# Conditional tiles as the last chunk of each expert, and one 512-column product for both parts of w2

## The chip, the core and the metric

The kernel runs on one core of one Trainium2 chip. The metric is device time in microseconds (us) of one launch. The time before is 896.36 us, the median of three runs (894.65 to 896.64).

## The reference

Two layers are computed and both results go into one output. The first is an RWKV-style attention block with a layer norm ahead of it; the second, with which the change has to do, is a mixture of experts behind another layer norm, whose result is added to the first layer's:

```python
h1 = jnp.einsum('ebcm,emh->ebch', dispatch, w1)
h3 = jnp.einsum('ebcm,emh->ebch', dispatch, w3)
expert_out = jnp.einsum('ebch,ehm->ebcm', jax.nn.silu(h1) * h3, w2)
final = jnp.einsum('ebcm,bsec->bsm', expert_out, combine_mask)
```

There are 8 experts, hidden size 256 (C), inner size 896 (F, 7 groups of 128), 4096 tokens, 2 experts for each token and room for 1280 rows (10 tiles of 128) in each expert. Everything is float32 on the outside.

## The kernel before

The program has two phases, written for five engines by hand, each as a list of instructions with semaphores. Phase A does the attention block, the router and the dispatch of rows to a buffer in HBM (`disp`), and the up products of expert 0's early tiles. Phase B (`phase_b`) does the experts.

**Precision.** A float32 product is made of three products of the type float32r: each operand is split into a high part and a low part (what is left over), and high x high, high x low and low x high are summed in PSUM. The weights of the next expert are split while this one is computed: ScalarE casts a piece of the raw weight `wraw` to the high part (`split_hi`, L1597), GpSimd subtracts for the low part (`split_lo`, L1540). There are 4 pieces (WP) for each of w1, w3 and w2, the matrices m = 0, 1 and 2.

**Tiles and chunks.** The 10 tiles of an expert lie in three chunks, `CHUNKS = [(0, 2), (2, 4), (6, 4)]` (first tile, number of tiles). Chunk 0 holds the last 256 rows of an expert's room. It is *conditional*: a count of the rows that the expert has (`taken`) is read into a register, and the chunk's up products are passed over where no row reaches it; its two down tiles are each decided in the same way (`where_taken`, L1440 to L1447). Where an arm is not taken the engine instead raises the semaphores that others wait for (`pass_over`). In the profiled execution experts 1, 3 and 5 take the chunk, with one down tile each.

**One expert on TensorE** (`step`, L1887). First the turn (transpose) of the conditional rows and `up(e, 0)`, if taken; then `up(e, 1)`, `down_rest(e, 0)` (the conditional down tiles), `up(e, 2)`, `down_chunk(e, 1)`, and `last_chunk(e)`: the four down tiles of chunk 2, with the turns of the next expert's rows between them. `up(e, c)` (L1802) makes 7 groups f of 12 products for w1 and w3, 512 columns wide in chunks 1 and 2 and 256 in chunk 0. `down(e, t)` (L1822) makes 21 products of 256 columns, three for each f:

```python
nc.tensor.matmul(py[j % 2][:, 0:C], a, hi[:, cut], start=(f == 0), stop=False)
nc.tensor.matmul(py[j % 2][:, 0:C], a, lo[:, cut], start=False, stop=False)
ins = nc.tensor.matmul(py[j % 2][:, 0:C], b, hi[:, cut], start=False, stop=(f == FT - 1))
```

**Behind the up products** stand, for each f, silu on ScalarE (`gated`, L1611), the product with the w3 half on VectorE (`hid`, L1734), its high part on ScalarE (`hh`, L1620) and its low part on VectorE (`hl`, L1742). `down` waits for the last low part of its chunk. Behind a down tile ScalarE scales it by the router's weight (`scale_out`, L1633) into one of four buffers `ysb`, and GpSimd adds it to the output with an indirect DMA (`add`, L1548).

**Expert 0** (`first`, L1874) starts with chunk 1, whose up products are in phase A: three down tiles, the turns of chunk 2's rows, the fourth down tile, then chunk 0 if taken, `up(e, 2)`, `down_rest`, `last_chunk`.

**Transfers.** SyncE's queue (`on_sync`, L1492) brings for the next expert, in this order: w1 and w3 (each when its buffer of `wraw` has been split), the rows `xtok` (when the turns of this expert's rows are all made or passed over: the semaphore `turned`; L1500), and w2 (L1507).

Of the kernel before, what the change touches and what calls it, by code (L numbers as in the profile page):

```python
# [161 lines left out]
def build(nc, x, maa, decay_row, decay_ch, u_row, wrT, wkT, wvT, wgT, woT, lnw, lnb, gateT, w1, w2, w3, out):  # L162
    disp = nc.dram_tensor("disp", [E * SLOTS, ROW], F32).ap()
    persist = ExitStack()
    with persist:
# [20 lines left out]
        whi = [[sb(f"whi0_{m}", [P, NW], F32R) for m in range(3)]]  # L186
        wlo = [[sb(f"wlo0_{m}", [P, NW], F32R) for m in range(3)]]
# [3 lines left out]
        with ExitStack() as ctx:  # L191
            first = phase_a(nc, *tensors(ctx), ctx, sem, ident, x, maa, decay_row, decay_ch, u_row, (wrT, wkT, wvT, wgT, woT),
                            lnw, lnb, gateT, disp, out, whi[0], wlo[0], wraw, expert_views(w1, w3, w2), taken, kept)
        with ExitStack() as ctx:
            sb2, ps2 = tensors(ctx)
            whi.append([sb2(f"whi1_{m}", [P, NW], F32R) for m in range(3)])
            wlo.append([sb2(f"wlo1_{m}", [P, NW], F32R) for m in range(3)])
            second = phase_b(nc, sb2, ps2, ctx, sem, ident, whi, wlo, wraw, w1, w2, w3, taken, disp, out, kept)
# [55 lines left out]

def expert_views(w1, w3, w2):
# [5 lines left out]
def phase_a(nc, sb, ps, ctx, sem, ident, x, maa, decay_row, decay_ch, u_row, weights, lnw, lnb, gateT, disp, out,  # L261
            whi, wlo, wraw, first_w, taken, kept):
# [160 lines left out]
    def piece_cut(i):  # L423
        return slice(i % WP * WPC, (i % WP + 1) * WPC)

# [45 lines left out]
    def on_gpsimd(pool):  # L471
# [76 lines left out]
        def weight_low(i):  # L548
            if 0 <= i < NPIECE:
                m, cut = i // WP, piece_cut(i)  # L550
                pool.wait_ge(whi_ready, i + 1)
                nc.gpsimd.tensor_tensor(wlo[m][:, cut], wraw[m % 2][:, cut], whi[m][:, cut].bitcast(F32),
                                        ALU.subtract).then_inc(wlo_ready, 1)
# [61 lines left out]
    def on_scalar(act):  # L615
# [108 lines left out]
        def weight_high(i):  # L724
            if 0 <= i < NPIECE:
                m, cut = i // WP, piece_cut(i)
                act.wait_ge(w_in[m % 2], 16 * (m // 2 + 1))
                nc.scalar.copy(whi[m][:, cut], wraw[m % 2][:, cut]).then_inc(whi_ready, 1)
# [413 lines left out]
    def on_tensor(pe):  # L1142
# [177 lines left out]
        def early_up(f):  # L1320
# [7 lines left out]
            for m, dst in ((0, early_p1[f % 2]), (1, early_p3[f % 2])):  # L1328
                for kt in range(KT):
                    wcut = slice(kt * F + f * P, kt * F + (f + 1) * P)  # L1330
                    nc.tensor.matmul(dst, whi[m][:, wcut], kept.xh[:, kt, early_cols], start=(kt == 0), stop=False)
                    nc.tensor.matmul(dst, whi[m][:, wcut], kept.xl[:, kt, early_cols], start=False, stop=False)
                    ins = nc.tensor.matmul(dst, wlo[m][:, wcut], kept.xh[:, kt, early_cols], start=False, stop=(kt == KT - 1))
# [68 lines left out]
def phase_b(nc, sb, ps, ctx, sem, ident, whi, wlo, wraw, w1, w2, w3, taken, disp, out, kept):  # L1402
# [17 lines left out]
    ffn_done, ysb_ready = sem("ffn_done"), sem("ysb_ready")  # L1420
# [34 lines left out]
    def run(eng, first, step):  # L1455
# [474 lines left out]
```

## Time and profile before

| | |
|---|---|
| median of 3 runs | 896.36 us |
| the profiled execution: its own time | 896.49 us |
| the profiled execution: span from first to last instruction | 894.8 us |
| TensorE (PE) busy | 846.2 us |
| ScalarE (ACT) busy | 489.2 us |
| VectorE (DVE) busy | 472.9 us |
| GpSimd (POOL) busy | 467.1 us |
| mean granted TensorE clock | 0.992 of full speed |

The span is shorter than the execution's own time by what lies ahead of the first and behind the last instruction. Phase B begins on TensorE at 364.71 us. PE is the row of matmuls, PEld that of weight loads, which overlap them; a name with a q behind it (PEldq, SPq) is the engine's sequencer or queue. A matmul's own duration includes time in which the next one already streams, so products are compared by the distance of their starts.

### The profile page before, as it was taken

Reading aid. Unit: us, or ns where it says so; the run is one execution under the profiler, and the core shown is the slowest. Engines: PE = TensorE matmul, PEld = TensorE weight load, DVE = VectorE, ACT = ScalarE, POOL = GpSimd, SP = SyncE. Lnnn points to the kernel's source line nnn. Section 1 sums busy time; section 2 is a strip of 40 time slices with the busy share of each in tenths; the row PEclk is TensorE's granted clock in tenths of the full one; section 3 lists DMA queues with packets and bytes.
Section 4 is the critical chain, followed back from the end, with each engine's and each line's share of the span. In section 5 each row is a group of like instructions: output and inputs, shape, how many; then the busy total and the mean of one; then the engine's idle time right before and its main releaser. Section 6 shows DMA issues by size and latency. Waiting matters only on the chain. (4 is left out here: it accounts for less than half of the span.)

```text
span 894.8 us, 18307 instructions
## 1 busy us (share of the span) xinstructions
PE 846.2 (95%) x6791; PEld 705.4 (79%) x6791; DVE 472.9 (53%) x1173; ACT 489.2 (55%) x876; POOL 467.1 (52%) x497
## 2 busy tenths in 40 slices
PE   3999999999999999889999999999999999999995
PEld 2777777777777777779889889879789889889885
DVE  6788788788888766343441442442351443342430
ACT  4578787777777779263542443443452444453331
POOL 4434766777767675564337355237346137447014
PEclk9999999999999999999999999999999999999998
DMA  5852132112111121546116236025417024314013
GB/s 154 320 193 67 50 102 67 62 56 80 38 38 38 38 98 53 170 150 139 42 42 118 86 92 111 5 78 89 112 48 137 22 72 92 82 42 54 7 19 42
DMA packets 50465, 73.93 MB, mean 83 GB/s; under 512 B 5056, under 2 KB 42176, under 8 KB 50368
## 3 DMA queue, kind: packets, MB, share of 16 engines
q1 hardware_dynamic: 35488, 53.46, 18.0%
q0 software_dynamic: 14592, 19.18, 12.5%
q8 instruction: 60, 0.98, 0.5%
q14 instruction: 37, 0.30, 0.1%
q10 hardware_dynamic: 288, 0.01, 0.0%
HBM read 38.41 MB, written 34.22 MB: 81 GB/s over the span
## 5 line engine op out<-in xcount | busy, mean ns | idle before, releaser
L1540 POOL TENSOR_TENSOR wlo<-wraw,whi 128x448 fp32r<-128x448 f32 x84 | 107.1, 1278 | 201.5 <-ACT whi L1597 201.5
L1817 PE MATMUL p<-xh,whi 128*128 128x512 f32 (+1 forms) x504 | 190.4, 378 | 7.3 <-DVE xl L1716 4.7
L1819 PE MATMUL p<-xh,wlo 128*128 128x512 f32 (+1 forms) x504 | 189.7, 376 | 0.0
L1818 PE MATMUL p<-xl,whi 128*128 128x512 f32 (+1 forms) x504 | 189.3, 376 | 0.0
L1734 DVE TENSOR_TENSOR hid<-gated,p 128x512 f32<-128x512 f32 (+1 forms) x126 | 81.1, 644 | 204.3 <-ACT gated L1611 204.3
L1548 POOL DMA_INDIRECT out<-ysb,index x80 | 126.0, 1575 | 85.2 <-ACT ysb L1633 55.1
L1611 ACT ACTIVATE gated<-p 128x512 f32<-128x512 f32 (+1 forms) x126 | 70.8, 562 | 179.7 <-PE p L1819 179.7
L1837 PE MATMUL py<-whi,hh 128*128 128x256 f32 x469 | 135.1, 288 | 6.2 <-DVE hl L1742 3.1
L1839 PE MATMUL py<-whi,hl 128*128 128x256 f32 x469 | 132.8, 283 | 0.0
L1838 PE MATMUL py<-wlo,hh 128*128 128x256 f32 x469 | 132.5, 283 | 0.0
L1817 PEld LDWEIGHTS p<-xh,whi 128*128 128x128 f32 x504 | 94.7, 188 | 27.4 <-DVE xl L1716 5.4
L1819 PEld LDWEIGHTS p<-xh,wlo 128*128 128x128 f32 x504 | 94.8, 188 | 19.0
L1818 PEld LDWEIGHTS p<-xl,whi 128*128 128x128 f32 x504 | 94.7, 188 | 18.7
L1633 ACT ACTIVATE ysb<-py,weight 128x256 f32<-128x256 f32 x67 | 31.7, 474 | 120.8 <-PE py L1839 100.8
L1837 PEld LDWEIGHTS py<-whi,hh 128*128 128x128 f32 x469 | 89.3, 190 | 7.3 <-DVE hl L1053 3.5
L927 DVE TENSOR_TENSOR attm<-pS,dmask 128x512 f32<-128x512 f32 x128 | 79.4, 682 | 27.8 <-PE pS L1218 23.5
L1742 DVE TENSOR_TENSOR hl<-hid,hh 128x512 fp32r<-128x512 f32 (+1 forms) x126 | 88.9, 706 | 3.7 <-ACT hh L1620 3.1
L1838 PEld LDWEIGHTS py<-wlo,hh 128*128 128x128 f32 x469 | 89.1, 190 | 0.4
L1839 PEld LDWEIGHTS py<-whi,hl 128*128 128x128 f32 x469 | 89.0, 190 | 0.0
L1716 DVE TENSOR_TENSOR xl<-pt,xh 128x512 fp32r<-128x512 f32 x33 | 22.7, 691 | 111.0 <-ACT xh L1603 111.0
L567 POOL DMA_INDIRECT disp<-row,slot_i x64 | 65.0, 1015 | 31.3 <-issue 14.3
L1620 ACT CAST hh<-hid 128x512 fp32r<-128x512 f32 (+1 forms) x126 | 72.8, 578 | 1.1 <-DVE hid L1734 1.1
(192 smaller groups left out, 1441.1 us busy)
## 6 DMA issues: line engine op xcount, KB each, us to landing
wraw<-in_w SPq DMA_DIRECT2D x24, 896.0 KB
disp<-wraw SPq DMA_DIRECT2D x16, 662.5 KB, 9.2
xtok<-disp SPq DMA_DIRECT2D x16, 530.0 KB, 4.5
x_ring<-in_x SPq DMA_DIRECT2D x16, 256.0 KB, 3.0
out<-x SPq DMA_DIRECT2D x16, 256.0 KB
xtok<-disp SPq DMA_DIRECT2D x8, 265.0 KB, 6.1
out<-ysb,index POOLq DMA_INDIRECT x80
disp<-row,slot_i POOLq DMA_INDIRECT x64
```

The lines of the kernel that those rows point to most:

```text
L927: nc.vector.tensor_tensor(attm[g][:], pS[:, :, g // 2, g % 2, :], group_mask(g), ALU.mult).then_inc(attm_ready[g], 1)
L1540: nc.gpsimd.tensor_tensor(wlo[e.const % 2][m][:, cut], wraw[k][:, cut], whi[e.const % 2][m][:, cut].bitcast(F32), ALU.subtract).then_inc(w ...
L1548: nc.gpsimd.indirect_dma_start(out, bass.IndirectOffsetOnAxis(ap=index[e.const % 2][:, t:t + 1], axis=0), ysb[j % NY][:], None, compute_op ...
L1620: nc.scalar.copy(hh[(u * NCH + q) % 2][:, f, 0:w], hid[k][:, 0:w]).then_inc(hh_ready, 1)
L1734: nc.vector.tensor_tensor(hid[k][:, 0:w], gated[k][:, 0:w], p3[k][:, 0:w], ALU.mult).then_inc(hid_ready, 1)
L1742: nc.vector.tensor_tensor(hl[s][:, f, 0:w], hid[k][:, 0:w], hh[s][:, f, 0:w].bitcast(F32), ALU.subtract).then_inc(hl_ready, 1)
L1817: nc.tensor.matmul(dst[:, 0:w], hi[m][:, wcut], xh[xcut], start=(kt == 0), stop=False)
L1818: nc.tensor.matmul(dst[:, 0:w], hi[m][:, wcut], xl[xcut], start=False, stop=False)
L1819: ins = nc.tensor.matmul(dst[:, 0:w], lo[m][:, wcut], xh[xcut], start=False, stop=(kt == KT - 1))
L1837: nc.tensor.matmul(py[j % 2][:, 0:C], a, hi[:, cut], start=(f == 0), stop=False)
L1838: nc.tensor.matmul(py[j % 2][:, 0:C], a, lo[:, cut], start=False, stop=False)
L1839: ins = nc.tensor.matmul(py[j % 2][:, 0:C], b, hi[:, cut], start=False, stop=(f == FT - 1))
```

## The change

Three things change, all in phase B's order and in how w2 is kept.

1. w2's high and low parts lie side by side (`Split.w2`, 128 x 7 x 2 x 256). In the tiles that are not conditional one product of 512 columns multiplies the high hidden values with both; the product of the low hidden values with the high weights stays. PSUM holds two halves of 256 columns. ScalarE scales the half with the low weights into `ysb` (semaphore `low_ready`), and VectorE multiplies the other half by the weight and adds it (`sum_out`, new). The conditional tiles keep three products and ScalarE alone.
2. In experts 0 to 6 the order of chunks is 1, 2, 0: `up(e, 1)`, the decision, in both of its arms `up(e, 2)` and the down tiles of chunk 1 (in the taken arm with the turn of the conditional rows ahead and `up(e, 0)` behind), `last_chunk(e)`, and `down_rest(e, 0)` last. The last expert keeps the order 0, 1, 2. ScalarE, VectorE and GpSimd follow.
3. In expert 0 two early down tiles instead of three stand ahead of the turns, one behind them, and the fourth behind `up(e, 2)`.

The pieces of w2 are cut through all 7 groups, 64 columns of each, where they were 448 contiguous ones. SyncE's list of transfers is the same.

```diff
--- before.py
+++ after.py
@@ -75,7 +75,7 @@
 def chunk_order(e):
 
-    return [EARLY, *(c for c in range(NCH) if c != EARLY)] if e.reg is None and e.const == 0 else list(range(NCH))
+    return [1, 2, 0] if e.const < E - 1 else [0, 1, 2]
...
+class Split:
+
+
+
+    def __init__(self, sb, k):
+        self.up = [[sb(f"w{part}{k}_{m}", [P, NW], F32R) for m in range(2)] for part in ("hi", "lo")]
+        self.w2 = sb(f"w2_{k}", [P, FT, 2, C], F32R)
+
+    def piece(self, part, m, q):
+
+        if m < 2:
+            return self.up[part][m][:, q * WPC:(q + 1) * WPC]
+        return self.w2[:, :, part, q * (C // WP):(q + 1) * (C // WP)]
+
+
+def raw_piece(raw, m, q):
+
+    if m < 2:
+        return raw[:, q * WPC:(q + 1) * WPC]
+    return raw[:].rearrange("p (f c) -> p f c", c=C)[:, :, q * (C // WP):(q + 1) * (C // WP)]
...
             j = ST * pair(e)[1] + q
             e.wait(pool, ysb_ready, ST, q + 1)
             pool.wait_ge(rows_in[0], 16)
+            if q == ST - REST and t < REST:
+
+                added_before(pool, e, ST // 2)
             nc.gpsimd.indirect_dma_start(
                 out, bass.IndirectOffsetOnAxis(ap=index[e.const % 2][:, t:t + 1], axis=0),
                 ysb[j % NY][:], None, compute_op=ALU.add).then_inc(added[j % NY], 16)
...
-            nc.scalar.activation(ysb[j % NY][:], py[j % 2][:, 0:C], ACT.Copy, scale=weight[e.const % 2][:, t:t + 1]).then_inc(ysb_ready, 1)
+            by = weight[e.const % 2][:, t:t + 1]
+            if t < REST:
+                e.wait(act, ysb_ready, ST, q)
+                nc.scalar.activation(ysb[j % NY][:], py[j % 2][:, 0:C], ACT.Copy, scale=by).then_inc(ysb_ready, 1)
+            else:
+                nc.scalar.activation(ysb[j % NY][:], py[j % 2][:, C:2 * C], ACT.Copy, scale=by).then_inc(low_ready, 1)
...
+        def sum_out(e, t):
+
+            q = tile_at(e, t)
+            j = ST * pair(e)[1] + q
+            e.wait(dve, low_ready, COMMON, t - REST + 1)
+            nc.vector.scalar_tensor_tensor(ysb[j % NY][:], py[j % 2][:, 0:C], weight[e.const % 2][:, t:t + 1], ysb[j % NY][:],
+                                           ALU.mult, ALU.add).then_inc(ysb_ready, 1)
+
...
-            hi, lo = whi[e.const % 2][2], wlo[e.const % 2][2]
+            w2, to = split[e.const % 2].w2, py[j % 2]
             for f in range(FT):
                 a, b = hh[s][:, f, off:off + P], hl[s][:, f, off:off + P]
-                cut = slice(f * C, (f + 1) * C)
-                nc.tensor.matmul(py[j % 2][:, 0:C], a, hi[:, cut], start=(f == 0), stop=False)
-                nc.tensor.matmul(py[j % 2][:, 0:C], a, lo[:, cut], start=False, stop=False)
-                ins = nc.tensor.matmul(py[j % 2][:, 0:C], b, hi[:, cut], start=False, stop=(f == FT - 1))
+                if t < REST:
+                    nc.tensor.matmul(to[:, 0:C], a, w2[:, f, 0, :], start=(f == 0), stop=False)
+                    nc.tensor.matmul(to[:, 0:C], a, w2[:, f, 1, :], start=False, stop=False)
+                    ins = nc.tensor.matmul(to[:, 0:C], b, w2[:, f, 0, :], start=False, stop=(f == FT - 1))
+                else:
+                    if f:
+                        nc.tensor.matmul(to[:, 0:C], b, w2[:, f, 0, :], start=False, stop=False)
+                    ins = nc.tensor.matmul(to[:], a, w2[:, f].rearrange("p h c -> p (h c)"), start=(f == 0), stop=(f == FT - 1))
+                    if not f:
+                        nc.tensor.matmul(to[:, 0:C], b, w2[:, f, 0, :], start=False, stop=False)
             ins.then_inc(ffn_done, 1)
 
         def down_chunk(e, c):
...
+        def with_rest_where_taken(e, between):
+
+
+            def up_rest():
+                turn(e, TB - 1)
+                between()
+                up(e, 0)
+
+            def no_rest():
+                pass_over(pe, e, (turned, TB - 1, TB, 1))
+                between()
+                pass_over(pe, e, (h_done, chunk_at(e, 0) * FT, HPE, FT))
+
+            where_taken(pe, e, COMMON, up_rest, no_rest)
 
...
         def first(e):
             t0, n = CHUNKS[EARLY]
-            for t in range(t0, t0 + n - 1):
+            for t in range(t0, t0 + n - 2):
                 down(e, t)
             for i in range(2, TB - 1):
                 turn(e, i)
-            down(e, t0 + n - 1)
+            down(e, t0 + n - 2)
             pe.wait_ge(taken_ready, 1)
-            rest_where_taken(e)
-            up(e, 2)
+
+            def second():
+                up(e, 2)
+                down(e, t0 + n - 1)
+
+            with_rest_where_taken(e, second)
+            last_chunk(e)
             down_rest(e, 0)
+
+        def step(e):
+            up(e, 1)
+
+            def second():
+                up(e, 2)
+                down_chunk(e, 1)
+
+            with_rest_where_taken(e, second)
             last_chunk(e)
-
-        def step(e):
+            down_rest(e, 0)
+
+        def last(e):
             rest_where_taken(e)
             up(e, 1)
             down_rest(e, 0)
@@ -1892,7 +2030,7 @@
             down_chunk(e, 1)
             last_chunk(e)
 
-        run(pe, first, step)
+        run(first, step, last)
```

The places that the prediction speaks of, in TensorE's list. First the start of expert 1, with the decision on the conditional chunk (L1443/L1444, in the change L1460/L1461). In the names p1 and p3 are the PSUM banks of the up products, py those of the down products, pt those of the turns. Before:

```order
L1838 MATMUL py1<-wlo0_2,hh0 128x256
L1839 MATMUL py1<-whi0_2,hl0 128x256
L1443 TENSOR_LOAD taken
L1444 COMPARE_AND_BRANCH
L1799 MATMUL pt1<-ident,xtok 128x128 [waits xl_ready,rows_in2]
L1799 MATMUL pt1<-ident,xtok 128x128 x3
L1817 MATMUL p1_1<-xh,whi1_0 128x256 [waits hid_ready,wlo_ready,xl_ready]
```

The change:

```order
L1920 MATMUL p3_1<-xl,whi1_1 128x512
L1921 MATMUL p3_1<-xh,wlo1_1 128x512
L1460 TENSOR_LOAD taken
L1461 COMPARE_AND_BRANCH
L1901 MATMUL pt1<-ident,xtok 128x128 [waits xl_ready,rows_in2]
L1901 MATMUL pt1<-ident,xtok 128x128 x3
L1919 MATMUL p1_0<-xh,whi1_0 128x512 [waits hid_ready,wlo_ready,xl_ready]
```

The decision has moved from behind the previous expert's down products to behind chunk 1's up products, and the products that follow the turn are chunk 2's of 512 columns, where they were the conditional ones of 256. This arm now also holds the down tiles of chunk 1 and `up(e, 0)`.

Next, the end of the conditional down tiles, `pass_over` with its wait for ffn_done. Before, in expert 1, between `up(e, 1)` and `up(e, 2)`:

```order
L1837 MATMUL py1<-whi1_2,hh1 128x256
L1838 MATMUL py1<-wlo1_2,hh1 128x256
L1839 MATMUL py1<-whi1_2,hl1 128x256
L1444 UNCONDITIONAL_BRANCH
L1446 UNCONDITIONAL_BRANCH [waits ffn_done] x2
L1817 MATMUL p1_1<-xh,whi1_0 128x512 [waits hid_ready,wlo_ready,xl_ready]
```

The change, at the end of expert 6 (behind its `last_chunk`), where the last expert's decision follows at once:

```order
L1940 MATMUL py1<-w2_0,hh0 128x256
L1941 MATMUL py1<-w2_0,hl0 128x256
L1461 UNCONDITIONAL_BRANCH
L1463 UNCONDITIONAL_BRANCH [waits ffn_done] x2
L1460 TENSOR_LOAD taken
L1461 COMPARE_AND_BRANCH
L1901 MATMUL pt1<-ident,xtok 128x128 [waits xl_ready,rows_in2]
L1901 MATMUL pt1<-ident,xtok 128x128 x3
```

The wait for ffn_done now stands behind the last product of the expert; behind experts 0 to 5 the next expert's `up(e, 1)` follows it, behind expert 6 the second decision.

## Rows read from the trace of the kernel before

**Rows 1.** The page's busy time of each engine (share of the span, instructions).
```profile
PE 846.2 (95%) x6791; PEld 705.4 (79%) x6791; DVE 472.9 (53%) x1173; ACT 489.2 (55%) x876; POOL 467.1 (52%) x497
```
**Rows 2.** Timeline of PE, expert 0: start, duration; in brackets the idle time before, releaser.
```profile
364.71 0.39 PE L1837 MATMUL py<-whi,hh 128*128 128x256 f32 x1 [3.04 <-DVE hl L1053]
...
377.11 0.28 PE L1839 MATMUL py<-whi,hl 128*128 128x256 f32 x1
377.98 0.47 PE L1817 MATMUL p<-xh,whi 128*128 128x512 f32 x1 [0.59 <-DVEq L1453]
...
401.30 0.39 PE L1837 MATMUL py<-whi,hh 128*128 128x256 f32 x1 [3.11 <-DVE hl L1742]
```
**Rows 3.** The same, first conditional product of experts 1 and 5 (first and last of three).
```profile
414.82 0.39 PE L1817 MATMUL p<-xh,whi 128*128 128x256 f32 x1 [1.55 <-DVE xl L1716]
...
690.32 0.39 PE L1817 MATMUL p<-xh,whi 128*128 128x256 f32 x1 [1.57 <-DVE xl L1716]
```
**Rows 4.** The same, first product of up(2) behind a conditional down tile, experts 1 and 5.
```profile
447.82 0.47 PE L1817 MATMUL p<-xh,whi 128*128 128x512 f32 x1 [0.54 <-POOL wlo L1540]
...
723.31 0.47 PE L1817 MATMUL p<-xh,whi 128*128 128x512 f32 x1 [0.53 <-POOL wlo L1540]
```
**Rows 5.** TensorE's reads of the register (taken) near 375 and 625, and a product behind.
```profile
L1443 PEldq TENSOR_LOAD <-taken x1: 497/497/497, 375.1 to 375.1; - x1
...
L1443 PEldq TENSOR_LOAD <-taken x1: 308/308/308, 624.7 to 624.7; - x1
...
627.26 0.47 PE L1817 MATMUL p<-xh,whi 128*128 128x512 f32 x1 [0.28 <-DVEq L1453]
```
**Rows 6.** Timeline of PE, 26 steps between down products, 20 between up products.
```profile
879.76 0.28 PE L1837 MATMUL py<-whi,hh 128*128 128x256 f32 x1
...
882.85 0.28 PE L1839 MATMUL py<-whi,hl 128*128 128x256 f32 x1
...
392.70 0.39 PE L1817 MATMUL p<-xh,whi 128*128 128x512 f32 x1
...
397.35 0.40 PE L1819 MATMUL p<-xh,wlo 128*128 128x512 f32 x1
```
**Rows 7.** Groups by line and shape (count, busy us, mean ns, idle before).
```profile
L908 DVE SCALAR_TENSOR_TENSOR mixed<-diff,maa_sb,xT 128x256 f32<-128x256 f32 x96 | 53.7, 613 | 0.0
L1734 DVE TENSOR_TENSOR hid<-gated,p 128x256 f32<-128x256 f32 x21 | 8.8, 421 | 19.9 <-ACT gated L1611 19.9
...
L1633 ACT ACTIVATE ysb<-py,weight 128x256 f32<-128x256 f32 x67 | 31.7, 474 | 120.8 <-PE py L1839 100.8 <-DMA out<-ysb,index 18.1 <-issue 1.9
```
**Rows 8.** Timeline, ACT's and POOL's last instructions.
```profile
885.30 0.47 ACT L1633 ACTIVATE ysb<-py,weight 128x256 f32<-128x256 f32 x1 [2.02 <-PE py L1839]
886.05 1.55 POOL L1548 DMA_INDIRECT out<-ysb,index  x1 [0.94 <-ACT ysb L1633]
```
**Rows 9.** Timeline of ACT and DVE behind the last up product of expert 0.
```profile
398.79 1.03 ACT L1597 CAST whi<-wraw 128x448 fp32r<-128x448 f32 x2
399.72 0.62 ACT L1620 CAST hh<-hid 128x512 fp32r<-128x512 f32 x1
400.37 0.87 DVE L1742 TENSOR_TENSOR hl<-hid,hh 128x512 fp32r<-128x512 f32 x1 [0.67 <-ACT hh L1620]
```
**Rows 10.** Landing of the row loads of 413 (three), the densest stretch, w2's first piece.
```profile
DMA to landing us min/median/max: 3.9/5.0/6.1
...
368.00:379.00 11.00, 10.40 (x80) 10.05 (x80) 1.44 (x4) 2.93 (x6) 5.53 (x4) 0.95 0.95 276
...
460.30 0.57 ACT L1597 CAST whi<-wraw 128x448 fp32r<-128x448 f32 x1
```
**Rows 11.** The page's DMA queues: instructions (packets, MB, share of 16 engines).
```profile
q8 instruction: 60, 0.98, 0.5%
```
**Rows 12.** Windows: busy us of PE, PEld, DVE, ACT, POOL, granted clock, DMA share, GB/s.
```profile
366.00:369.00 3.00, 3.00 (x16) 3.00 (x16) 0.00 (x0) 0.23 (x1) 0.00 (x1) 0.50 0.17 51
401.00:404.00 3.00, 2.70 (x22) 2.70 (x23) 0.85 (x2) 0.00 (x0) 2.81 (x2) 1.00 0.21 29
```

More of the change, by code:

```diff
@@ L185, in build @@
         kept = Kept(nc, sb)
[L186 to L187 removed]
+        split = [Split(sb, 0)]
         wraw = [sb(f"wraw{k}", [P, NW]) for k in range(2)]
@@ L725, in weight_high @@
             if 0 <= i < NPIECE:
-                m, cut = i // WP, piece_cut(i)
+                m, q = i // WP, i % WP
                 act.wait_ge(w_in[m % 2], 16 * (m // 2 + 1))
-                nc.scalar.copy(whi[m][:, cut], wraw[m % 2][:, cut]).then_inc(whi_ready, 1)
+                nc.scalar.copy(split.piece(0, m, q), raw_piece(wraw[m % 2], m, q)).then_inc(whi_ready, 1)
         def turned1(b):
@@ L1453, in pass_over, with run @@
             eng.sem_inc(s, by)
-    def run(eng, first, step):
+    def run(first, step, last):
         first(At(0))
-        step(At(1))
-        for e in range(2, E):
+        for e in range(1, E - 1):
             step(At(e))
+        last(At(E - 1))
     def banks():
@@ L1578, in step @@
             added_before(pool, e, 0)
-            for t in range(ST):
+            for q, t in enumerate(tile_order(e)):
                 add(e, t)
-                if t == ST - 3 and (e + 1).valid(E):
+                if q == ST - 3 and (e + 1).valid(E):
                     keep_index(e + 1)
-        run(pool, first, step)
+        run(first, step, step)
         added_before(pool, At(E), 0)
@@ L1596, in split_hi @@
                 e.wait(act, ffn_done, ST, -ST)
-            nc.scalar.copy(whi[e.const % 2][m][:, cut], wraw[(3 * u + m) % 2][:, cut]).then_inc(whi_ready, 1)
+            nc.scalar.copy(split[e.const % 2].piece(0, m, q), raw_piece(wraw[(3 * u + m) % 2], m, q)).then_inc(whi_ready, 1)
         def turn_hi(e, i):
@@ L1708, in free_hidden @@
             past.wait(eng, ffn_done, ST, tiles_done(past, q % NCH))
-        run(act, first, step)
+        run(first, step, last)
     def on_vector(dve):
@@ L1775, in first, with second, last @@
             dve.sem_inc(rows_used, 1)
-            rest_where_taken(e)
-            hidden(e, 2)
-            next_rows(e + 1)
-        def step(e):
+            def second():
+                hidden(e, 2)
+                sum_out(e, t0 + n - 1)
+            with_rest_where_taken(e, second)
+            last_chunk(e, True)
+        def step(e):
+            hidden(e, 1)
+            def second():
+                hidden(e, 2)
+                sum_chunk(e, 1)
+            with_rest_where_taken(e, second)
+            last_chunk(e, True)
+        def last(e):
             rest_where_taken(e)
@@ L1783, in step @@
             hidden(e, 2)
-            if (e + 1).valid(E):
-                next_rows(e + 1)
-        run(dve, first, step)
+            sum_chunk(e, 1)
+            last_chunk(e, False)
+        run(first, step, last)
     def on_tensor(pe):
@@ L1875, in first @@
             t0, n = CHUNKS[EARLY]
-            for t in range(t0, t0 + n - 1):
+            for t in range(t0, t0 + n - 2):
                 down(e, t)
@@ L1893, in step @@
             last_chunk(e)
-        run(pe, first, step)
+        run(first, step, last)
     return on_sync, on_gpsimd, on_scalar, on_vector, on_tensor
```

115 lines of the change are left out of this document (77 added, 38 removed).

## The prediction

> **What bounds the kernel now.** I read the engine shares of the page first. They show TensorE busy 95% of the span and no other engine above 55% [rows 1], so time can come only from TensorE's products or from its gaps. Next I read TensorE's own order of time for what stands in brackets behind a product, which is the gap before it. In the second phase these gaps are few. Expert 0 waits 3.11 us for the last low part of the hidden values before its last four tiles [rows 2]. Each of the three experts that take the conditional tiles (1, 3 and 5) waits 1.55 to 1.57 us for VectorE's xl before the first conditional product [rows 3]. After the one conditional down tile that each of them has, TensorE drains and restarts with 0.53 to 0.54 us lost in the first and the last of them [rows 4]. Two more places lose 0.59 and 0.28 us behind a decision that is read but not taken [rows 2, 5]. Then I took the pitch of products from start to start: 26 products of 256 columns take 3.09 us, 118.9 ns each; 20 of 512 columns take 4.65 us, 232.5 ns each [rows 6].
>
> **Part 1: one 512-column product.** A down tile has 7 triples of 256-column products; the 64 tiles that are not conditional become 7 pairs, one of 256 columns and one of 512. The columns streamed are the same 768. A triple costs 3 x 118.9 = 356.6 ns, a pair 118.9 + 232.5 = 351.4 ns: 5.2 ns less, and 448 of them give **2.3 us**. No row shows the two widths in turn. One bound is no gain, if the time goes by columns alone. The other comes from the slope of the same rows: (232.5 - 118.9) / 256 = 0.444 ns a column, 768 columns at that are 341 ns, which would give 15.8 ns x 448 = 7.1 us. I take 2.3, because it uses each width's own row. The Trainium skill (TensorE: Matmul & The Clock Gate, "Back-to-back issue gap") gives a gap of N/2.4 + 2.5 ns, so dropping one product of three would save 2.5 ns a triple and 1.1 us in all; its gaps of 109 and 216 ns are shorter than both measured pitches, so I keep the rows.
>
> The price is a VectorE step: ScalarE scales the low half (256 columns, 474 ns as before), VectorE multiplies the high half from PSUM and adds. The nearest VectorE rows are 421 ns for a two-input product and 613 ns for a scalar-tensor-tensor of this size [rows 7]; I take 0.5. For 63 of the 64 tiles it is hidden: a tile takes 2.5 us, its two PSUM banks alternate, and 0.47 + 0.5 us with two hand-overs are over long before the tile after next begins. Queued behind it on VectorE are the next expert's turned rows and weights, which have a tile's time each. Without that cover each tile would lose 0.6 us. At the very end there is no cover: ScalarE's scale at 885.30 released the last scatter at 886.05 [rows 8], and VectorE now stands between. That costs 0.5 + 0.1 = **0.6 us**.
>
> **Part 2: the order in expert 0.** Its last early tile moves behind the second chunk's up products. The wait of 3.11 us is a chain behind the last up product: silu, two weight pieces (1.03 us), the high part at 399.72, the low part at 400.37 [rows 9]. None of that gets shorter, but 21 products (2.5 us) now lie inside it. About 0.6 us stays. Gain **2.5 us**.
>
> **Part 3: the conditional tiles last (experts 0 to 6).** The turn of the conditional rows now has chunk 2's up products and chunk 1's down products (30 us) between it and its use, so the three gaps of rows 3 go: **4.7 us**. They are replaced as follows.
>
> - The down part of the conditional chunk now ends each expert. Not taken, it waits for the expert's own last product (ffn_done) before the next expert's up products can be issued. The same wait costs 0.53 to 0.54 us in the taken case today [rows 4]. Taken experts keep it; experts 0, 2 and 4 are new: 3 x 0.54 = **1.6 us lost**. The existing 0.28 us [rows 5] goes into it: 0.3 gained.
> - Between experts 6 and 7 two decisions follow each other, because the last expert keeps the old order. The second is read only after the first has drained TensorE. From the reading of the register to the next product rows show 377.98 - 375.1 = 2.9 us [rows 2, 5] and 627.26 - 624.7 = 2.6 us [rows 5]. Today TensorE's queue hides most of this; here the queue is empty. **2.7 us lost**.
> - The decision after up(1) is hidden. The read at 375.1 is 17 products ahead of the last one issued (377.1, 118.9 ns apart); at 512 columns 17 products are 3.9 us, more than 2.9.
> - At the end of a taken arm TensorE jumps over the other arm, under 256-column products, with only 2 us of queue. I put 0.1 us on each of three: **0.3 us**, below by nothing.
> - Transfers: the rows of expert e+1 are requested only after up(1), and w2 of e+1 stands behind them in SyncE's queue. Rows need 3.9 to 6.1 us to land; the densest stretch moved 276 GB/s, so rows and w2 together (2.2 MB) need some 8 to 9 us and are there about 10 us into up(2) at worst [rows 10]. The first piece of w2 is taken 12.5 us into up(2) (447.82 to 460.30) [rows 4, 10]. Hidden by some 2.5 us.
> - GpSimd issues the two conditional scatters after the others, 1.55 us each [rows 8]. Behind them stand the next expert's low weight parts, which start two up groups (5.6 us) later. Its new wait for this expert's first five scatters asks for ones issued over 10 us before: nothing.
> - The pieces of w2 are now cut in runs of 64 elements on ScalarE and GpSimd. If GpSimd took half as long again, its four pieces would still end before the down products that read them. Nothing.
>
> **The sum.** Gains 2.3 + 2.5 + 4.7 + 0.3 = 9.8; losses 0.6 + 1.6 + 2.7 + 0.3 = 5.2; net 4.6 us. The profiled execution took 896.49 us (span 894.8), so 891.9; it lies 0.13 above the median of the three runs, so 891.8 us.
>
> **Rivals.**
> (A) *The wide product gives nothing* because only columns count. For: columns are unchanged, and the pitch of both widths is near proportional. Against: the intercept of rows 6 is positive. 891.8 + 2.3 = **894.1 us**.
> (B) *Long jumps become visible: slower.* The arms now hold the second chunk's up and down products, so that the decision of experts 1 to 6 jumps over 226 products where it jumped over 88, and a taken arm ends by jumping over 140 where it jumped over none. If the instructions there must first be brought in, each jump costs x more. The page's instruction queue moved 60 blocks at 0.5% of 16 engines' span: 0.005 x 16 x 894.8 / 60 = 1.2 us a block [rows 11]. The three arm-end jumps pay all of x, the six early ones what exceeds 3.9 - 2.7 = 1.2. The gain is gone when 3x + 6(x - 1.2) = 4.6, at x = 1.3 us. With one block 895.4; with a request in front of it, x = 2, 6.0 + 4.8 = 10.8 lost, **902.6 us**. Against: today's jump over 88 products costs about the same in all its places, and ScalarE and VectorE make theirs without a gap. The Trainium skill (Runtime: NRT & Kernel Launch, "Instruction fetch mechanics") says that a branch whose target lies outside the two 16 KiB pages held forces a fetch before execution goes on. By that rule the longer jumps here would often miss, and the time would be this rival's; no row of this trace shows a miss.
> (C) *w2 arrives late.* ScalarE would stand at the piece and TensorE two groups later. It decides where rows and w2 land over 12.5 us into up(2); at 2 us late in six experts it gives 891.8 + 12 = 903.8, at 1 us **897.8 us**. Against: the margin above.
> (D) *Better:* the wide product by the slope gives 4.8 more, or the second decision before expert 7 is cheaper: **888 us**.
>
> A gap of 3.04 us before 364.71 was followed by products at the 1.2 GHz level [rows 2, 12], and one of 3.11 us was not. The new gap before expert 7 may have such a stretch behind it, at up to 1.7 us; the range holds it.
>
> **How the numbers follow.** Forecast 0.55 (its own range 890 to 893.8), A 0.14, B 0.17 (half of it near 895.4), C 0.04, D 0.10. A measurement of this kernel can tell about 0.2%, 1.8 us. Faster by more: the forecast, D and most of A, 0.76. Within it: the rest of A and the mild part of B, 0.10. Slower: the rest of B, and C, 0.14. The range 888.5 to 897.5 leaves out the far end of D and the hard cases of B and C.
>
> **What would show it.** No gap for xl before the first conditional product; no gap over 1 us before expert 0's last four tiles; seven gaps near 0.55 us between experts but near 2.7 before the last; pairs at 351 ns; VectorE's 64 new steps near 0.5 us with nobody waiting but the last scatter. Wrong would be: gaps of a microsecond at the first product after a taken arm or at up(2) (B), ScalarE standing for a transfer at a w2 piece (C), or pairs at 357 ns (A).

## The result and the profile after

The changed kernel takes 894.77 us (median of 20 runs), the kernel before, measured beside it, 896.6 us (median of 20): a ratio of 0.9973, 95% interval 0.9960 to 0.9985. In a second comparison, beside the experiments, it was 0.9970 (0.9957 to 0.9984). The change makes the kernel faster by 0.3%, about 2 us. The profiled execution has a span of 893.8 us, 1.0 below that of before, where the prediction had 4.6 less. All ratios are of fast runs, which leaves out one execution of e7 (1673.9 us), whose cause is open.

The page's shares, which answer to [rows 1]:

```profile
PE 844.0 (94%) x6343; PEld 680.8 (76%) x6343; DVE 502.7 (56%) x1237; ACT 489.0 (55%) x876; POOL 465.1 (52%) x497
```

TensorE has the 448 products less and VectorE the 64 sums more. Next the timeline of TensorE in expert 0 and at the ends of experts 0, 1, 4 and 6 (start, duration, idle time before in brackets, releaser), which answers to [rows 2 to 5]:

```profile
379.24 0.50 PE L1919 MATMUL p<-xh,whi 128*128 128x512 f32 x1 [3.72 <-issue]
...
404.15 0.50 PE L1945 MATMUL py<-w,hh 128*128 128x512 f32 x1 [0.68 <-DVEq L1470]
...
415.91 0.47 PE L1919 MATMUL p<-xh,whi 128*128 128x512 f32 x1 [0.30 <-PEq L1470]
...
490.17 0.47 PE L1919 MATMUL p<-xh,whi 128*128 128x512 f32 x1 [0.54 <-PEq L1470]
...
687.26 0.47 PE L1919 MATMUL p<-xh,whi 128*128 128x512 f32 x1 [0.30 <-PEq L1470]
...
824.71 0.47 PE L1919 MATMUL p<-xh,whi 128*128 128x512 f32 x1 [2.08 <-DVEq L1470]
```

The wait of expert 0 before its last four tiles is down from 3.11 to 0.68 us, and the three waits for xl are gone. A boundary behind an expert that passes the conditional tiles over loses 0.30 us, behind one that takes them 0.54. Two gaps stand out: 2.08 us before expert 7, and 3.72 us before expert 0's first up(2) product, where [rows 2] had 0.59. The gap of 3.72 us is followed by a stretch at the 1.2 GHz level, as the first window shows; in the second window, expert 0's last four tiles, the granted clock is full (windows: busy us of PE, PEld, DVE, ACT and POOL, granted clock, DMA share, GB/s):

```profile
380.00:383.00 3.00, 3.00 (x8) 2.34 (x8) 0.00 (x0) 0.00 (x0) 0.00 (x0) 0.50 0.87 251
404.00:407.00 3.00, 2.85 (x17) 2.51 (x18) 1.09 (x3) 0.18 (x2) 2.66 (x2) 1.00 0.26 32
```

The pairs, by the first and the last of the eight one-of-a-tile products (L1947) of the last expert, then the groups, then the end of the kernel:

```profile
864.22 0.28 PE L1947 MATMUL py<-w,hl 128*128 128x256 f32 x1
...
881.33 0.28 PE L1947 MATMUL py<-w,hl 128*128 128x256 f32 x1
```
```profile
L1945 PE MATMUL py<-w,hh 128*128 128x512 f32 x448 | 162.3, 403 | 3.7 <-DVE hl L1070 3.0 <-DVEq L1470 0.7
...
L1807 DVE SCALAR_TENSOR_TENSOR ysb<-py,weight,ysb 128x256 f32<-128x256 f32 x64 | 30.9, 483 | 99.6 <-ACT ysb L1657 97.5 <-issue 2.1
```
```profile
883.75 0.47 ACT L1657 ACTIVATE ysb<-py,weight 128x256 f32<-128x256 f32 x1 [1.98 <-issue]
884.26 0.48 DVE L1807 SCALAR_TENSOR_TENSOR ysb<-py,weight,ysb 128x256 f32<-128x256 f32 x1 [1.97 <-ACT ysb L1657]
885.02 1.55 POOL L1568 DMA_INDIRECT out<-ysb,index  x1 [0.91 <-DVE ysb L1807]
```

Seven tiles lie between the two products: 17.11 us, 2.444 a tile, 349.1 ns a pair. The same seven tiles before took 17.44 us (865.17 to 882.61, by starts), 2.491 a tile. The sum is 0.48 us, and from ScalarE's last scale to the last scatter it is now 1.27 us, where [rows 8] had 0.75.

### The profile page after: what moved, and what is told of

Same layout as the page of the kernel before. It is cut to its first block and busy times, and to the rows that moved or that the text cites. A ratio compares the mean times of both kernels' runs of the same rounds, so it can differ in the third digit from the quotient of the medians.

```text
span 893.8 us, 17491 instructions
## 1 busy us (share of the span) xinstructions
PE 844.0 (94%) x6343; PEld 680.8 (76%) x6343; DVE 502.7 (56%) x1237; ACT 489.0 (55%) x876; POOL 465.1 (52%) x497
## 5 line engine op out<-in xcount | busy, mean ns | idle before, releaser
L1945 PE MATMUL py<-w,hh 128*128 128x512 f32 x448 | 162.3, 403 | 3.7 <-DVE hl L1070 3.0
L1557 POOL TENSOR_TENSOR wlo<-wraw,whi 128x448 fp32r<-128x448 f32 x56 | 71.1, 1272 | 103.3 <-ACT whi L1616 103.3
L1944 PE MATMUL py<-w,hl 128*128 128x256 f32 x384 | 108.3, 282 | 0.0
L1945 PEld LDWEIGHTS py<-w,hh 128*128 128x128 f32 x448 | 83.1, 190 | 18.9 <-DVE hl L1070 3.5
L1807 DVE SCALAR_TENSOR_TENSOR ysb<-py,weight,ysb 128x256 f32<-128x256 f32 x64 | 30.9, 483 | 99.6 <-ACT ysb L1657 97.5
L1944 PEld LDWEIGHTS py<-w,hl 128*128 128x128 f32 x384 | 72.7, 189 | 2.9
L1168 PE MATMUL pB<-mixed,w_in_sb 128*128 128x256 f32 x256 | 62.2, 386 | 0.0
L1557 POOL TENSOR_TENSOR w<-wraw,w 128x448 fp32r<-128x448 f32 x28 | 36.1, 1291 | 37.1 <-ACT w L1616 37.1
```

What stands on the lines that cost most here:

```text
L1557: nc.gpsimd.tensor_tensor(to.piece(1, m, q), raw_piece(wraw[k], m, q), to.piece(0, m, q).bitcast(F32), ALU.subtract).then_inc(wlo_ready, 1)
L1944: nc.tensor.matmul(to[:, 0:C], b, w2[:, f, 0, :], start=False, stop=False)
L1945: ins = nc.tensor.matmul(to[:], a, w2[:, f].rearrange("p h c -> p (h c)"), start=(f == 0), stop=(f == FT - 1))
```

## The experiments

The kernel before took 883.4 us in the first comparison (e1 to e4) and 897.2 and 899.6 us in the two later ones (e5 to e8, e9 to e11). The 14 us lie in phase A, which no experiment edits (phase B began at 350.4 to 352.1 us in e1 to e4, at 364.0 to 366.9 in all the others). So only ratios to the kernel before of the same comparison are set side by side. A second measure leaves phase A out: the time from phase B's first down product to the last instruction, in the one profiled execution of each kernel.

| kernel | phase B, us |
|---|---|
| before | 530.1 |
| changed (again in e5) | 528.5 (528.1) |
| e1, the product alone | 547.9 |
| e2, the order alone | 534.8 |
| e3, short jumps in expert 0 | 524.5 |
| e4, short jumps in experts 0 to 6 | 522.8 |
| e6, before with a long jump | 537.0 |
| e7, e1 with VectorE's decision first | 533.9 |
| e8, all together | 520.6 |
| e9, e2 with short jumps | 523.4 |
| e10, e11, one decision moved before expert 7 | 527.6, 528.3 |

### The two halves of the change, each alone (e1, e2)

e1 keeps the order of before and takes the wide product with VectorE's sum. Against the changed kernel:

```diff
-    return [1, 2, 0] if e.const < E - 1 else [0, 1, 2]
+    return [1, 0, 2] if e.const == 0 else [0, 1, 2]
...
+        def step(e):
+            rest_where_taken(e)
+            up(e, 1)
             down_rest(e, 0)
-
-        def step(e):
-            up(e, 1)
...
-            with_rest_where_taken(e, second)
+            up(e, 2)
+            down_chunk(e, 1)
             last_chunk(e)
-            down_rest(e, 0)
```

> The order of the kernel before, with the 512-column product and VectorE's sum. If the pair costs what the changed kernel's tiles show (one tile 45 ns shorter than before, 64 tiles), 2.9 us are gained and 0.6 lost behind the last tile: 2.3 us below before, near 894.2. The gaps of before stand: about 0.6 us at expert 0's first up(2) product, 3.1 before its last four tiles, 1.55 three times for xl. Rival: that the wide product gives nothing and the whole gain is the order's; then it is 0.6 us slower than before.

Measured: 899.6 us, ratio **1.0186** (1.0163 to 1.0209), 16 us slower. e2 has the new order, with three 256-column products and ScalarE alone:

```diff
         def sum_out(e, t):
-
+            return
...
-                if t < REST:
+                if True:
                     nc.tensor.matmul(to[:, 0:C], a, w2[:, f, 0, :], start=(f == 0), stop=False)
```

> The new order, with three 256-column products and ScalarE alone as before. If the order's gain is eaten by the jump over the longer arm in expert 0, the gap of about 3.7 us before the first product of expert 0's up(2) and a stretch at the 1.2 GHz level behind it stand here too, and the time is within 1 us of before (895.5 to 897.5). Rival: if the gap came of VectorE's new sums or of the w2 layout, it is gone here, and the order gives its forecast 2 to 3 us (near 893.5).

Measured: 889.68 us, ratio **1.0076** (1.0051 to 1.0102), 6 us slower. Neither half does alone what I expected, and their losses do not add up to the changed kernel's gain: each half removes something of what the other costs. The timeline of e1's TensorE shows what its half costs:

```profile
365.50 0.48 PE L1905 MATMUL p<-xh,whi 128*128 128x512 f32 x1 [2.41 <-DVEq L1470]
...
405.37 0.39 PE L1905 MATMUL p<-xh,whi 128*128 128x256 f32 x1 [1.99 <-DVE xl L1758]
...
481.57 0.47 PE L1905 MATMUL p<-xh,whi 128*128 128x512 f32 x1 [2.09 <-DVEq L1470]
...
622.52 0.47 PE L1905 MATMUL p<-xh,whi 128*128 128x512 f32 x1 [2.08 <-DVEq L1470]
```

Four boundaries cost 2.06 to 2.09 us (481.57, 622.52, 765.23, 828.11), where before had one of 0.28 and three of 0.1 or none; the three waits for xl grew from 1.56 to 1.99. And behind four of these seven gaps TensorE went to 1.2 GHz for a while; behind 622.52, for one. It did so behind expert 0's wait of 3.12 us as well (the second window), where before had kept the full clock behind the same wait:

```profile
624.00:627.00 3.00, 3.00 (x9) 2.35 (x8) 0.00 (x0) 0.00 (x0) 0.00 (x0) 0.52 1.06 335
...
389.00:392.00 3.00, 3.00 (x10) 2.61 (x11) 0.36 (x1) 0.00 (x0) 2.54 (x3) 0.50 0.28 57
```

By starts, each of the four cost 1.4 to 1.5 us (84 conditional products in 11.68 us behind one, in 10.18 behind another gap without it), and the one in expert 0, which lasted longer, 2.6 us. The account against the profile of before is 4 x 2.08 - 0.28 for the boundaries, 3 x 0.43 for xl, 5.9 for four stretches, 1.8 + 2.6 in expert 0, - 3.0 for the pairs and + 0.5 at the end: 17.1 of the 17.9 us by which phase B is longer (16.2 us by the medians).

What ends each gap is the raise of a semaphore by VectorE (L1470 is `pass_over`). Its sequencer's rows at the place where the changed kernel has this gap too, before expert 7, follow, with the timeline beside them:

```profile
822.67 0.47 ACT L1657 ACTIVATE ysb<-py,weight 128x256 f32<-128x256 f32 x1 [1.87 <-PE py L1945]
823.18 0.48 DVE L1807 SCALAR_TENSOR_TENSOR ysb<-py,weight,ysb 128x256 f32<-128x256 f32 x1 [1.65 <-ACT ysb L1657]
823.58 0.17 DVE L1774 TENSOR_SCALAR weight<-xtok 128x10 f32<-128x10 f32 x1
```
```profile
L1460 DVEq TENSOR_LOAD <-taken x1: 303/303/303, 823.9 to 823.9; - x1
...
L1470 DVEq EVENT_SEMAPHORE  x3: 21/21/21, 824.4 to 824.7; - x3
```

The chain is: last product, scale, sum, copy of the weights, VectorE's own read of the register (823.9), its `pass_over` (824.4), TensorE's up(1) at 824.71. TensorE's own read was at 822.8. In the kernel before, VectorE had no work behind the last product of an expert, and its decision was over by up(1), or 0.28 us late at most ([rows 5]). The sum puts the decision behind that product. With the old order up(1) needs it at once. In the new order it stands behind up(1), and TensorE does not stand for it, except before expert 7, which keeps the old order.

e2's loss has another form (timeline of its TensorE, then the decision of expert 0 and the branch near the end of expert 1's taken arm):

```profile
365.27 0.77 PE L1918 MATMUL p<-xh,whi 128*128 128x512 f32 x1 [4.31 <-PEq L1470]
...
463.76 0.41 PE L1900 MATMUL pt<-ident,xtok 128*128 128x128 f32 x2 [1.63 <-issue]
...
738.56 0.41 PE L1900 MATMUL pt<-ident,xtok 128*128 128x128 f32 x2 [2.03 <-issue]
...
816.29 0.47 PE L1918 MATMUL p<-xh,whi 128*128 128x512 f32 x1 [1.49 <-PEq L1470]
```
```profile
L1461 PEldq COMPARE_BRANCH  x1: 5682/5682/5682, 359.3 to 359.3; - x1
...
L1461 PEldq COMPARE_BRANCH  x1: 3354/3354/3354, 460.2 to 460.2; - x1
```

The branches in front of the first three gaps take 3.4 to 5.7 us, where in the kernel before the longest of its 22 took 0.36. The 1.49 us before expert 7 are of another kind: there two decisions follow each other behind a drained queue, as I had predicted, and no branch is long.

### Shorter jumps (e3, e4, e9)

Two short decisions in place of the one long arm, so that `up(e, 2)` and the down tiles stand outside; in e3 in expert 0, in e4 in experts 0 to 6, with ScalarE and VectorE alike:

```diff
+        def in_two_decisions(e, between):
+            where_taken(pe, e, COMMON, lambda: turn(e, TB - 1), lambda: pass_over(pe, e, (turned, TB - 1, TB, 1)))
+            between()
+            where_taken(pe, e, COMMON, lambda: up(e, 0), lambda: pass_over(pe, e, (h_done, chunk_at(e, 0) * FT, HPE, FT)))
...
-            with_rest_where_taken(e, second)
+            in_two_decisions(e, second)
```

> The changed kernel, but expert 0 makes two short decisions (one on the turn, one on the conditional up products) with up(2) and the down tile between them and outside of the arms. If the instruction queue had to be filled again behind the long jump, the 3.7 us gap falls to 0.9 or less and the 1.2 GHz stretch behind it goes: 4 to 5 us below the changed kernel, near 890.5, with up to 0.6 us at the second decision. Rival: if the gap is a wait for data (rows, xl, weights in a busy DMA stretch), it stays and the time is that of the changed kernel, 894.8, or a little more.

Measured: 877.15 us, ratio **0.9930** (0.9908 to 0.9952).

> The same in experts 0 to 6. Beside e3 the jumps of experts 2 and 6 that took over 3.5 us become short, which gives 0.9 us; the second decision of the experts that are not taken stands behind down products with 2 us of queue ahead, where 0.3 us each are lost. So within 1 us of e3. If jumps over 84 products miss as well, it is slower than e3 by 1 us or more in each of experts 2, 4 and 6.

Measured: 874.7 us, ratio **0.9902** (0.9882 to 0.9922); the two intervals overlap, so that the step from e3 to e4 may be the 1 us that I expected or several. In both, the product before up(2) and the up(2) product follow each other without a gap:

```profile
360.39 0.40 PE L1959 MATMUL py<-w,hh 128*128 128x512 f32 x1
360.63 0.40 PE L1933 MATMUL p<-xh,whi 128*128 128x512 f32 x1
```

e3 still has three long branches, in experts 2, 4 and 6 (3.38, 3.68 and 3.48 us), each behind up(1), where the queued products cover nearly all of it; in e4 none of its 32 takes over 0.36 us. The gap before expert 7 is 2.07 us in both. e9 is e2 with the two short decisions:

> The new order with three 256-column products and ScalarE alone, as in 'new order only', but with two short decisions in experts 0 to 6. Theory (that version's loss was code behind long jumps): the 4.3 us before expert 0's first up(2) product and the 1.6 and 2.0 us at the ends of the taken arms go, with a 1.2 GHz stretch behind the first, and the time falls from 1.0076 to 0.995 to 0.998 of before; this is then what the order is worth by itself. Rival (the order itself costs it): it stays at 1.005 or above.

Measured: 892.01 us, ratio **0.9912** (0.9895 to 0.9928). The gaps named went, all of them, and the longest branch is 0.36 us. The gain from e2 (1.6%, some 14 us) is larger than I expected: I had summed the gaps (8.0 us) and not the two 1.2 GHz stretches of e2, of which e9 has none ahead of its end, and e2's profiled execution was 2.5 us below its median. In the profiles its phase B is 6.6 us shorter than that of before. So the order by itself is worth 0.9%, once its jumps are short; e9 and e4 differ by the product alone, and their intervals overlap. What the product gives behind the order is too small for these runs (by rows: 3.0 us, less 0.5 at the end, less 2.07 - 1.34 = 0.7 before expert 7).

### The changed kernel again, and a long jump in the kernel before (e5, e6)

> The changed kernel as it is, beside the kernel before on the same chip as the experiments. If the loss of 3.72 us before expert 0's first up(2) product plus the half-clock stretch behind it (1.6 us) is what the two short decisions took away, this one stands 5 to 6 us above 'short decisions in expert 0', so at 0.998 to 1.000 of the kernel before. If the two short decisions gained for another reason, the gap before up(2) is gone here too or the ratio lies near 0.993. Another placement of the program on another chip may move the gap's size, not its place.

Measured: 894.74 us, ratio 0.9970 (0.9957 to 0.9984). The gap before up(2) is 3.80 us. The step to e3, 0.4%, is some 3.5 us, less than the 5.4 that gap and stretch add up to, but within the two intervals. The profiles show where 1.5 us of the difference went: in e3 the gap before expert 7 has a 1.2 GHz stretch behind it (168 products in 40.81 us), in the changed kernel it has none (39.27 us). So the gap and its stretch go where the two decisions are made short, and a stretch elsewhere hides a part of it in e3's time.

e6 is the kernel before, with transposes that never run at the end of expert 0's arm:

```diff
             def up_rest():
                 turn(e, TB - 1)
                 up(e, 0)
+                if e.const == 0:
+                    for _ in range(97):
+                        nc.tensor.transpose(pt[0][:, 0:P], xtok[:, 0, 0:P], ident[:])
```

> The kernel before, with 97 transposes added at the end of expert 0's conditional arm, which is not taken: they are jumped over, never executed. The jump is 185 products long where it was 88. Theory (code beyond the jump has to be brought in): the gap before expert 0's first up(2) product grows from 0.6 to 3 to 4.5 us with a 1.2 GHz stretch behind it, and the time rises by 3 to 6 us. Rival (the gap comes from the order of waits, not from the length of the arm): 0.6 us as before, and no change in time.

Measured: 902.6 us, ratio **1.0045** (1.0026 to 1.0064), 4 us slower (5.4 by the medians) by instructions that are not executed. The timeline of its TensorE, its branch, and a window behind:

```profile
379.95 0.77 PE L1817 MATMUL p<-xh,whi 128*128 128x512 f32 x1 [3.36 <-PEq L1453]
```
```profile
L1444 PEldq COMPARE_BRANCH  x1: 4549/4549/4549, 374.9 to 374.9; - x1
```
```profile
380.00:382.00 2.00, 2.00 (x5) 1.61 (x6) 0.00 (x0) 0.00 (x0) 0.00 (x0) 0.50 0.86 131
```

The branch was 358 ns in the kernel before. The order of waits is unchanged, so the added instructions alone make the gap: the jump is longer and its target lies elsewhere in the program, and this run does not tell the two apart. By starts they cost 2.8 us of gap and 2.7 at 1.2 GHz behind it; 1.5 more stand behind the wait of 3.11 us before the last four tiles, where before had none.

### VectorE's decision ahead of its sum (e7, e10, e11), and all together (e8)

VectorE decides first, and does the last tile's sum in either arm; in e7 in e1's kernel for every expert, in e10 in the changed kernel for the last one:

```diff
+        def last_sum(past):
+            sum_out(past, ST - 1)
+            keep_weight(past + 1)
...
             def hidden_rest():
+                if e.const > 0:
+                    last_sum(e - 1)
                 turn_lo(e, TB - 1)
                 hidden(e, 0)
+            def no_rest():
+                n = chunk_at(e, 0) * FT
+                pass_over(dve, e, (xl_ready, TB - 1, TB, 1), (hid_ready, n, HPE, FT), (hl_ready, n, HPE, FT))
+                if e.const > 0:
+                    last_sum(e - 1)
```

> The order of before with the 512-column product, as in the first experiment, but VectorE takes its decision for the next expert before the last tile's sum, and does this sum inside either arm. Theory (VectorE's decision behind the last sum is what TensorE's next up products wait for): the four gaps of 2.1 us between experts 1/2, 3/4, 5/6 and 6/7 fall to at most 0.6 us, and the time falls by 8 to 12 us against the first experiment (8.4 us of gaps and up to 3 us of 1.2 GHz stretches behind them). The gap before expert 0's first up(2) product (2.4 us) and the three for xl (2.0 us) stay. Rival (the wide product itself or its weight load brings the gaps): they stay at 2.1 us and so does the time.

Measured: 899.88 us, ratio **1.0014** (0.9994 to 1.0033), 1.7% below e1's. No gap is left at any of the four boundaries, and the waits for xl are back at 1.56 us:

```profile
421.44 0.38 PE L1917 MATMUL p<-xh,whi 128*128 128x256 f32 x1 [1.56 <-DVE xl L1758]
```

The theory holds; I had the size too small (some 15 us by the ratios, 14.0 in phase B, against 8 to 12): all four 1.2 GHz stretches of e1 from expert 1 on went, 5.9 us for my 3, and the longer waits for xl, which I had expected to stay. Expert 0's 2.40 us stays: there too VectorE decides behind a sum. With the 1.2 GHz stretches behind it and behind the wait of 3.11 us in the same expert it takes more than the pairs give back, so that the product alone is not faster here either.

e10 and e11 put my prediction's step for expert 7 (TensorE's second decision behind a drained queue) against VectorE's. e11 moves TensorE's and ScalarE's decision:

```diff
             last_chunk(e)
+            if e.const == E - 2:
+                rest_where_taken(e + 1)
             down_rest(e, 0)
```

> The changed kernel with one edit: VectorE takes its decision for the last expert before the last sum of expert 6. Theory (the gap of 2.07 us before expert 7 is VectorE's, whose decision stands behind the sum): it falls to what TensorE's own second decision leaves, 1.5 us as in 'new order only'. Rival (the step of my prediction: TensorE's second decision behind the drained queue makes the gap): it stays at 2.07 us.

> The changed kernel with the other edit: TensorE and ScalarE take their decision for the last expert before the conditional down tiles of expert 6, so no second decision stands behind the drained queue; VectorE's stays behind the last sum. Theory (VectorE): the gap before expert 7 stays at 2.0 to 2.1 us. Rival (TensorE's second decision): it falls to 0.3 to 0.6 us.

Measured in e10 and then in e11:

```profile
825.22 0.47 PE L1931 MATMUL p<-xh,whi 128*128 128x512 f32 x1 [1.23 <-PEq L1470]
```
```profile
824.96 0.47 PE L1921 MATMUL p<-xh,whi 128*128 128x512 f32 x1 [2.08 <-DVEq L1470]
```

VectorE's decision sets the length of the gap; with VectorE's moved ahead, TensorE's second one leaves 1.2 us (1.3 and 1.5 in e9 and e2, which have no sum). Their single times (896.39 and 895.94 us beside 899.58 of before) tell no difference of 0.8 us.

e8 joins e4, e10 and e11, and lets the very last tile do without the wide product:

```diff
+def alone(e, t):
+
+    return e.const == E - 1 and t == ST - 1
...
-                if t < REST:
+                if t < REST or alone(e, t):
                     nc.tensor.matmul(to[:, 0:C], a, w2[:, f, 0, :], start=(f == 0), stop=False)
```

> The changed kernel with two short decisions in experts 0 to 6, VectorE's decision for the last expert before the last sum, TensorE's and ScalarE's decision for it ahead of the conditional down tiles of expert 6, and the very last tile with three 256-column products and ScalarE alone. Theory: the gap before expert 7 falls from 2.07 to about 0.5 us (1.5 us gained), the tail loses VectorE's 0.6 us; so about 2 us below 'short decisions in experts 0 to 6', at 0.987 to 0.990 of before. Rival (the gap before expert 7 has a third cause): it stays near 2 us and the time gains 0.6 us at most.

Measured: 886.42 us, ratio **0.9871** (0.9850 to 0.9892), 1.3% below the kernel before and 1% below the changed one. The gap before expert 7, and the end:

```profile
817.08 0.47 PE L1953 MATMUL p<-xh,whi 128*128 128x512 f32 x1 [0.30 <-PEq L1475]
...
876.16 0.47 ACT L1660 ACTIVATE ysb<-py,weight 128x256 f32<-128x256 f32 x1 [2.01 <-issue]
876.90 1.55 POOL L1573 DMA_INDIRECT out<-ysb,index  x1 [0.42 <-ACT ysb L1660]
```

From the scale to the last scatter it is 0.74 us again.

## Why the prediction was right, and where a step failed

The sign and the range held: faster by 0.3%, where I had forecast 0.5%. The number itself, 894.8 us, lies outside of what I gave the forecast alone (890 to 893.8). It lies between rival A (894.1), which the pairs refute, and the mild case of rival B (895.4). That the error stayed at some 3 us is in part luck: I had left out 6.2 us of cost, smaller terms came out 2.4 us better than I had them, and no 1.2 GHz stretch stood behind the gap before expert 7, as one did in e3. Step by step, in the profiled executions:

- **The product: right.** 349.1 ns a pair where I had 351.4. Against 355.9 for a triple in the same tiles it is 6.8 ns and 3.0 us in all, where I had 5.2 ns and 2.3 us. Rival A is refuted.
- **The end: right.** 0.5 us for 0.6; the sum takes 0.48.
- **Expert 0's wait: right.** 3.11 to 0.68 us, 2.4 gained for 2.5.
- **The waits for xl: right.** 4.7 us gone.
- **The boundaries: right in place, too large in size.** 0.30 us each behind experts 0, 2 and 4, not 0.54: 0.9 us for 1.6.
- **Expert 7: the wrong mechanism with nearly the right size.** I wrote that "the second is read only after the first has drained TensorE" and took 2.7 us. It costs 2.08, and what ends it is VectorE's decision behind its new sum. In part 1 I had looked at what is queued behind the sum ("turned rows and weights") and left out the decision there.
- **"The decision after up(1) is hidden": nearly.** In experts 2 and 6 the branch took 3.8 and 3.5 us, just about what the queue of 512-column products holds. The 168 products of up(1) and up(2), in the middle of which it stands, took 39.87 and 39.47 us there, where before had 39.27 and 39.13.
- **Rival B: right in mechanism, counted in the wrong place.** This is the step that failed. (A small slip beside it: the decision jumps over 88 + 140 = 228 products, not 226.) I had x between 1.2 and 2 us; a branch that misses takes 3.3 to 3.8 us. I charged it to the three arm ends and to six early jumps, and left out expert 0, whose decision stands behind down products with 2 us of queue. In the changed kernel it is expert 0 that pays: 3.1 us more of gap and 1.6 of the clock stretch behind (up(2)'s 84 products took 21.18 us from 379.24 where they had taken 19.61). The arm ends cost nothing; in e2, with other code lengths, two of the three cost 1.6 and 2.0. That expert 0's gap is the jump's is what e3, e4 and e9 show, where it goes with the long jump.
- **Rival C: not seen.** No gap of TensorE in the changed kernel's second phase has a transfer as its releaser.

The sum of these: -3.0 + 0.5 - 2.4 - 4.7 + 0.9 - 0.3 (the wait of [rows 5], which went into it) + 2.1 + 3.1 + 1.6 + 0.9 (experts 2 and 6) = -1.3 us, and phase B began 0.5 us later: -0.8, measured -1.0. Against the forecast of -4.6, expert 0's 4.7 us and 1.5 elsewhere (experts 2 and 6, the start, the wait) were missing, and smaller terms (the pairs, the boundaries, expert 7, the arm ends, the end) came out 2.4 us better than forecast.

## What to carry to other kernels

Before you put a step on an engine, follow what stands behind it on that engine, decisions and semaphore raises too: a 0.48 us sum cost some 15 us (e1 against e7) because a decision was queued behind it. Keep conditional arms short in instructions, or make the decision while more work is queued than a miss takes: common work inside both arms lengthens the jump. And test the parts of a change alone: here either half was slower by itself, and with the causes removed the gain was three to four times as large.

## What the runs showed of the hardware

- **A jump that misses costs 3.3 to 3.8 us, and more under load.** The profile's instruction queue (q8) brings blocks of 16,384 bytes, and one such packet is all that the DMA moved in e2 from 460.3 to 463.5 (the queue's row for that window; below it the changed kernel's branches of experts 2 and 0):

```profile
q8 instruction: 1, 0.02, 1.9%
...
L1461 PEldq COMPARE_BRANCH  x1: 3817/3817/3817, 506.2 to 506.2; - x1
...
L1461 PEldq COMPARE_BRANCH  x1: 358/358/358, 373.0 to 373.0; - x1
```

In e2 the branch began at 460.2, the block was moved from 461.20 to 462.18, and the branch ended at 463.6: 1.0 us ahead of the transfer, 1.0 in it, 1.4 behind. With DMA otherwise idle seven such branches (five of e2, two of the changed kernel) took 3.32 to 3.82 us; in expert 0, where the weights were being loaded, 4.55 us (e6, 281 GB/s until the block moved) and 5.68 us (e2, 352 GB/s). In the changed kernel's expert 0 the branch itself took 358 ns, and the sequencer stood behind it: its last raise was at 373.5, the block was moved only at 377.05, when the load of weights (381 GB/s until then) eased, and the product came at 379.24. That the load delays it fits all three; no run here changed the load alone. The Trainium skill (Runtime: NRT & Kernel Launch, "Instruction fetch mechanics") says that instructions come in blocks of 16 KiB, and that a taken branch to a target outside of the two blocks held has to wait until the target's block is fetched. The traces agree on the block (16,384 bytes) and on the wait (3.32 to 3.82 us with one block in it); how many blocks are held no run here shows directly.
- **Which jump misses depends on the whole program's layout.** A jump over 88 products missed in none of the places before. The long arms missed in experts 0, 2 and 6 of the changed kernel, and in 2, 4 and 6 in e3, whose arms in experts 1 to 6 are the same and which differs in expert 0 alone. So an edit in one place moves the misses in others.
- **A gap of 2 us can cost another 1.5.** Of e1's seven gaps of 2.0 to 2.1 us from expert 1 on, four were followed by products at 1.2 GHz, and of the same gap before expert 7 that of e3, but not those of the changed kernel, e4, e5 and e11; none of the gaps of 1.5 to 1.6 us in phase B was, in any of the kernels. The wait of 3.1 us before expert 0's last four tiles was followed by such a stretch in e1, e6 and e7 and not in before. What decides it is open.
- **14 us between comparisons** lie in phase A of one and the same code. Between e4 and e5 they grow little by little over most of phase A, and do not come at one place. What causes them is open.
